# An attention and feed-forward kernel on one core: another order and other senders at the head of each batch element, and four banks for half of the score tiles by key

## What is computed

```python
def bi_wkv(r, k, v, w, u, time_emb):          # two of them: one before attention, one before the FFN
    tf = sigmoid(sum(time_emb, -1))
    decay = exp(-exp(w)) * (0.5 + 0.5 * tf)
    ek = exp(minimum(k, 30)); ekv = ek * v
    nf, df = scan(a = a * decay + ekv_t), scan(b = b * decay + ek_t)      # over the tokens
    nb, db = the same scans in reverse
    euk = exp(minimum(u + k, 30))
    num = nf + nb - ekv + euk * v
    den = df + db - ek + euk
    return sigmoid(r) * num / maximum(den, 1e-8) * (0.8 + 0.2 * tf)

def attention(h, w_qkv, w_o):                 # 16 heads of 32, causal, softmax over the keys
    q, k, v = split(h @ w_qkv.T)
    probs = softmax(where(causal, q @ k.T / sqrt(32), min))
    return (probs @ v) @ w_o.T

def ffn(x, w_gate, w_up, w_down):             # inputs and weights quantized in blocks of 32
    return mx(silu(mx(x) @ mx(w_gate).T) * (mx(x) @ mx(w_up).T)) @ mx(w_down).T

x = x + attention(bi_wkv(x, fside, fside, w1, u1, cond), w_qkv, w_o)
x = x + ffn(bi_wkv(x, fside, fside, w2, u2, cond), w_gate, w_up, w_down)
```

## Time and profile before

| | us |
|---|---|
| median of 3 runs | 870.95 (870.93 to 872.39) |
| the profiled execution | 873.02 |
| its span | 871.3 |
| DVE busy | 752.6 (86%) |
| PE busy | 741.5 (85%) |
| ACT busy | 507.6 (58%) |

### The profile page before, as it was taken

How to read it: one execution, slowest core, us unless ns; L and a number is a source line. 1 busy time by engine, 2 the same in 40 slices (tenths; PEclk the granted TensorE clock), 3 DMA queues, 4 the chain that set the end, 5 groups by cost and what they waited for, 6 DMA issues and landing times.

```text
span 871.3 us, 10845 instructions
## 1 busy us (share of the span) xinstructions
PE 741.5 (85%) x3964; PEld 393.8 (45%) x4001; DVE 752.6 (86%) x1070; ACT 507.6 (58%) x754; POOL 72.6 (8%) x149
## 2 busy tenths in 40 slices
PE   4567668699889999798899998988899998999785
PEld 1222223355544444454444443555444444557674
DVE  4899999999999879789998798899898888834887
ACT  4966655376874575378764663677736636443440
POOL 1000001202000003011000021110000211200000
PEclk9786687899999999999999999999999999999998
DMA  9623210557100005654010047460100355500001
GB/s 325 266 96 109 101 63 23 125 124 182 39 30 21 1 12 128 190 163 102 13 37 1 13 97 205 113 166 14 37 1 12 83 153 135 126 1 1 1 2 48
DMA packets 31252, 73.06 MB, mean 84 GB/s; under 512 B 5856, under 2 KB 6880, under 8 KB 29408
## 3 DMA queue, kind: packets, MB, share of 16 engines
q1 hardware_dynamic: 19584, 46.67, 17.9%
q0 software_dynamic: 6144, 16.79, 8.1%
q10 hardware_dynamic: 5472, 8.92, 3.2%
HBM read 34.61 MB, written 4.19 MB: 45 GB/s over the span
## 4 chain that ended last, share of the span: by engine, by line
DVE 44%; PE 26%; issue 13%; ACT 8%; DMA 3%; SPq 3%; POOL 1%; ACTq 0%; DVEq 0%
PE bank L1627 9%; DVE negmax L1077 5%; DVE num L983 3%; SPq L337 3%; PE bank L1520 2%; DVE fn L969 2%; PE bank L1464 2%; PE bank L1482 2%; PE bank L1392 2%; ACT region L583 2%; DVE ratio L1116 2%; PE bank L1426 2%; PE bank L1493 2%; DMA stacks<-rows 1%; DVE den L994 1%
## 5 line engine op out<-in xcount | busy, mean ns | idle before, releaser
L1077 DVE TENSOR_REDUCE negmax<-bank 128x4 f32<-128x512 f32 (+2 forms) x96 | 97.8, 1036 | 31.9 <-PE bank L1429 19.5
L583 ACT ACTIVATE region<-bank 128x384 f32<-128x384 f32 (+1 forms) x192 | 93.2, 526 | 46.3 <-PE bank L1467 45.4
L1464 PE MATMUL bank<-stacks 128*128 128x512 f32 (+3 forms) x256 | 103.2, 411 | 18.8 <-ACT region L583 13.4
L1400 PE MATMUL bank<-h,wqkv 128*128 128x512 f32 x256 | 115.5, 605 | 0.0
L1426 PE MATMUL bank<-stacks 128*128 128x128 f32 (+3 forms) x256 | 78.6, 402 | 7.1 <-DVE negmax L1077 4.9
L337 POOL DMA_DIRECT2D stacks<-rounded_rows x64 | 34.7, 550 | 521.1 <-DVE ratio L1116 321.6
L1400 PEld LDWEIGHTS bank<-h,wqkv 128*128 128x128 f32 x256 | 49.4, 195 | 58.1 <-issue 57.2
L1466 PE MATMUL bank<-maxrow,pick 128*128 128x384 bf16 (+3 forms) x236 | 73.2, 310 | 0.0
L1464 PEld LDWEIGHTS bank<-stacks 128*128 128x128 f32 x256 | 50.3, 197 | 45.0 <-ACT region L583 27.4
L1392 PE MATMUL bank<-wqkv,h 128*128 128x512 f32 x128 | 62.7, 635 | 4.7 <-DVE h L1017 4.7
L1682 PE MATMUL bank<-region,ident 128*128 128x512 f32 x64 | 49.2, 930 | 12.0 <-DVE identb L928 12.0
(11 more groups left out here) (197 smaller groups left out, 1558.5 us busy)
## 6 DMA issues: line engine op xcount, KB each, us to landing
stacks<-rounded_rows SPq DMA_DIRECT2D x64, 128.0 KB, 4.5
stacks<-rounded_rows POOLq DMA_DIRECT2D x64, 128.0 KB, 5.0
stacks<-rows SPq DMA_DIRECT2D x64, 128.0 KB, 2.5
stacks<-rows POOLq DMA_DIRECT2D x64, 128.0 KB, 2.6
kt<-in_fside ACTq DMA_DIRECT2D x30, 256.0 KB, 3.3
region<-in_w_gate SPq DMA_DIRECT2D x4, 1024.0 KB, 11.3
h<-in_x SPq DMA_DIRECT2D x4, 1024.0 KB, 5.7
xt<-in_x SPq DMA_DIRECT2D x4, 1024.0 KB, 5.6
```

The source lines that it names most:

```text
L583: nc.scalar.activation(probs[:, i, P_AT[tiles[0]]:P_AT[tiles[0]] + columns], key_bank(g, n)[:, 0:columns], ACT.Exp, scale=SCALE).then_inc( ...
L1077: nc.vector.tensor_reduce(o, scored, AX_X, ALU.max, negate=True).then_inc(max_taken, 1)
L1400: mm = nc.tensor.matmul(qk_banks(g)[s][:, :], wqkv[:, j, C * s + P * g:C * s + P * g + P], h[:, j, :], start=(j == 0), stop=(j == CJ - 1))
L1464: nc.tensor.matmul(o, ks[s][:, i, P * t:P * t + P], qs[s][:, i, P * t:T], start=True, stop=False, skip_group_check=True)
```

## The change

Six edits. **(1)** Head 1 of group 1 is stacked by ACT instead of SP, in all four turns, behind `low_parts`; SP sends head 0 alone, and does so ahead of the stores of the element before, which follow it. **(2)** DVE at the head: the xt additions go ahead of `add_own(b, 9)`, `forward(b, 2, ...)` behind the fourth maximum. **(3)** PE at the head: the first projection is cut in two halves around slots 0 and 1, the second stands behind slots 2 and 3, the values behind slots 4 and 5. **(4)** ACT: `copy_maxima(b, 0)` ahead of the two `weigh`, `copy_values(b, (0,))` behind the first two exponentials; a table load ahead of `load_k` and `floored`; `cap_exp(b, 7)` behind the twelfth exponential of group 3 instead of the ninth. **(5)** Score tiles by key of groups 1 and 2 go from the fifth on (n of 4 or more) round banks 4, 5, 6, 7 instead of 4, 5 (HALF_RING is 4). **(6)** Unit 6, the first on bank 6, waits for `normed`, units 8 to 11 for the exponential of the unit four before.

```diff
-            return bank[(4, 5, 0, 1, 2, 3)[n % 6]] if g == GROUPS - 1 else bank[4 + n % 2]
+            if g == GROUPS - 1:
+                return bank[(4, 5, 0, 1, 2, 3)[n % 6]]
+            return bank[4 + (n % 4 if g and n >= HALF_RING else n % 2)]
...
@@ block.sync @@
             def turn(b, more):
                 sp.wait_ge(down_ready, 1 + b)
-                stack(sp, b, 1, 0, 2)
+                stack(sp, b, 1, 0, 1)
                 if b:
+                    store(b - 1, True)
                     sp.wait_ge(stored, b * (16 * CJ))
                     sp.dma_start(xt[:, :, :], x[b]).then_inc(x_in, 16)
...
@@ block.scalar @@
             def turn(b, more):
                 high_parts(b, 1)
                 low_parts(b, 1)
+                act.wait_ge(down_ready, 1 + b)
+                stack(act, b, 1, 1, 2)
                 load_k(b, 1)
                 reciprocals(b, 1)
                 own_exp(b, 2)
                 copy_raw(b, 2)
                 late_high_parts(b)
+                copy_maxima(b, 0)
                 weigh(b, 2, 0)
                 weigh(b, 2, 1)
-                copy_maxima(b, 0)
+                exps(b, 0, 0, 2)
                 copy_values(b, (0,))
-                exps(b, 0, 0, 5)
+                exps(b, 0, 2, 5)
...
-                exps(b, 3, 2, 9)
+                exps(b, 3, 2, 12)
                 cap_exp(b, 7)
-                exps(b, 3, 9, 12)
...
@@ block.tensor, scores_by_key @@
+                elif g and HALF_RING <= n:
+                    free = n - 2 if n == HALF_RING + 1 or n == HALF_RING else n - 4
+                    if n == HALF_RING + 2:
+                        pe.wait_ge(normed, b * GROUPS + g)
+                    if n not in (HALF_RING + 2, HALF_RING + 3):
+                        pe.wait_ge(p_ready, b * (GROUPS * UNITS) + g * UNITS + free + 1)
```

More of the change, by code:

```diff
@@ L379, in turn, with store @@
                     stack(sp, b + 1, 0, 0, 2)
+            def store(b, more):
                 for j in range(CJ):
@@ L392, in _ @@
                 turn(b, b + 1 < B)
+            store(B - 1, False)
             sp.wait_ge(weights_in, 32)
@@ L673, in turn @@
                 copy_maxima(b, 2)
+                if more:
+                    table(6)
                 load_k(b, 4)
                 floored(b, 4)
-                if more:
-                    table(6)
                 exps(b, 2, 0, 1)
@@ L1231, in turn @@
             def turn(b, more):
[L1232 to L1241, removed]
+                maxima(b, 0, 0)
+                maxima(b, 0, 1)
+                if b == 0:
                     backward(b, 1, 1)
                     add_own(b, 1)
[L1244 to L1247, removed]
+                maxima(b, 0, 2)
+                maxima(b, 0, 3)
+                forward(b, 2, 0)
+                forward(b, 2, 1)
                 maxima(b, 0, 4)
@@ L1373, in turn @@
                 backward(b, 9, 1)
-                add_own(b, 9)
                 for j in range(CJ):
@@ L1377, in turn @@
                     nc.vector.tensor_tensor(xt[:, j, :], bank[j][:, :], xt[:, j, :], ALU.add).then_inc(out_ready, 1)
+                add_own(b, 9)
             for b in range(B):
@@ L1395, in project_values, with project_qk @@
                     mm.then_inc(v_ready, 1)
-            def project_qk(b, g, s):
-                for j in range(CJ):
+            def project_qk(b, g, s, first=0, last=CJ):
+                for j in range(first, last):
                     mm = nc.tensor.matmul(qk_banks(g)[s][:, :], wqkv[:, j, C * s + P * g:C * s + P * g + P], h[:, j, :],
-                                          start=(j == 0), stop=(j == CJ - 1))
-                mm.then_inc(qk_ready, 1)
+                                          start=(j == 0), stop=(j == CJ - 1), skip_group_check=True)
+                if last == CJ:
+                    mm.then_inc(qk_ready, 1)
             def leave_low(b, g, s):
@@ L1733 @@
 VALUE_ORDER = (2, 3, 0, 1)
+HALF_RING = 4
 SLOT_BEHIND = ({1: 0, 2: 1, 4: 2, 7: 3, 9: 4, 11: 5}, {2: 2, 5: 3, 8: 4, 11: 5})
```

7 lines of the change are left out of this document (4 added, 3 removed).

## The result

| | before | changed | ratio |
|---|---|---|---|
| median of four runs each, same chip | 871.11 us (870.93 to 872.39) | 857.15 us (856.61 to 857.56) | 0.9836, 95% interval 0.9819 to 0.9853 |
| profiled execution | 873.02 us, span 871.3 | 857.56 us, span 855.8 | |
| a later chip, median of 9 and 4 runs | 873.13 us | 857.33 us (856.94 to 857.74) | 0.9818, 0.9804 to 0.9832 |

The kernel is 14 us faster by the first pair of medians and 15.8 us faster by the second; the two profiled spans differ by 15.5 us.

What follows compares the result with a forecast made beforehand. The prediction took the wait for SP's stacks to bound the heads and DVE to bound groups 1 to 3. Gains of 4.6 + 4.35 + (3.3 + 1.6) = 13.85 us off 870.95 gave 857.1 us, range 852.5 to 862.5.

Steps and rivals of the forecast that it cites:

- The sum of 13.85 us: Whole kernel: gains of 4.6 in b = 1, 4.35 in b = 2 and 3.3 + 1.6 in b = 3.
- The end of the last landing: Head of b = 1: group 1's last stack lands at 356.5 instead of 360.26, between 355.7 and 359.0.
- ACT's issues: Head: ACT issues four stacks at 0.6 us each, 2.4 us, with bounds of 2.3 to 10 us for four.
- The rival that the prediction put beside it: Heads: the bytes bound, last stack lands at 359.0, each head gives 1.3 to 1.7 less: 861.6 us, chance 0.16.
- Slot 4 of group 1: Head of b = 1: DVE reaches it at 373.5 instead of 378.69, PE being the later one; gain 5.2 us.
- The 0.6 us taken off b = 1: First slot of group 2: b = 1 would wait for PE as b = 2 does (0.57 us), leaving 4.6 us.
- The 1.15 us of `cap_exp`: Group 3 of b = 2: DVE's wait for the sum goes once `cap_exp` no longer stands between the exponentials, 1.15 us.
- The slow clock of b = 1: Behind b = 1's head: TensorE's clock at 0.50 in 366 to 368 goes; b = 2 and b = 3 have none.
- Four banks: Units 8 and 11 of two groups in the last turn find a free bank, 0.4 us each: 1.6 us.
- b = 0 at nothing: Turn b = 0: no stores, DVE is bound behind PE's first tile; gain 0, between -0.5 and +1 us.
- Copying the maxima first, at nothing: ACT: `copy_maxima` ahead of `weigh` moves work inside ACT's slack and gives nothing of its own.
- The slower rival: Heads: ACT's queue takes the place of SP's, issues of 2.50 us, last landing at 362.3: 875.6 us, chance 0.03.

Runs made afterwards that it cites:

- order alone: Changed kernel with the queues of before (stores first, then all eight of SP's stacks, none from ACT): 871.46 us, ratio 0.9987.
- queues alone: Kernel before with ACT sending head 1 of group 1 and SP's stack ahead of the stores, engines' order and two banks kept: 865.86 us, ratio 0.9920.

## Why the prediction was right, and where it wasn't

Forecast 857.1, measured 857.15. The agreement to 0.05 us is luck. The sum of 13.85 us was short of the 15.5 us by which the spans differ: for the profiled execution it gives 859.2 us, and that took 857.56, 1.6 less. The medians met because the three runs of before had theirs 2.1 us under the profiled execution, where the changed kernel has 0.4; the two errors cancelled. On the later chips the median of before was 872.7 to 873.1, and on the one of them that ran the changed kernel the gain was 15.8 us. The mechanism of the heads, from which most of the sum comes, is what the runs bear out.

**The end of the last landing** (356.5 out of 355.7 to 359.0): the landing released ACT at 356.50. Right, and the step on which most of the gain rests. The order alone gave nothing and the queues alone 6.9 us; together they gave 15.8. So about half of the gain comes only with both. Each takes one of two limits of the same stretch away: with the queues alone DVE still waits 5.82, 5.54 and 4.37 us in the three heads, with both 3.2 in each; with the order alone the landing holds it. That isn't the whole of it: the order alone also made the landing later, and of what the changed kernel has over the queues alone 1.6 us are the four banks. The prediction summed DVE's work against both limits at once, which is why it did not fall into this; the expectation of the order alone, which priced it as a part of the sum, did.

**ACT's issues** (0.6 us each, 2.4 for four): 3.08 us in b = 1, 0.74 at the median. Too low by a quarter, without effect. Whether ACT matters as a sender at all the prediction left open. The Trainium skill (DMA: Bandwidth & Descriptors, Issuing engines are not separate DMA queues) has it that several senders save only issuing time. With the stacks first, 857.46 against 857.33 us agrees. The rival that the prediction put beside it, 861.6 us, did not come: standing ahead of the stores was enough by itself for the early landing.

**Slot 4 of group 1.** Forecast 373.5 in b = 1, measured 373.54; the additions began at 344.57 instead of 344.95, the first tile by key came at 360.78 by the chain (forecast 360.5), and PE was the later one, as said. In b = 2, taking off what b = 1 had gained, 548.98 + 5.18 = 554.16 (forecast 554.0), in b = 3 724.41 + 10.23 = 734.64 (734.8).

**The 0.6 us taken off b = 1** for a wait at the first slot of group 2 (0.57 in b = 2): wrong. Neither b = 1 nor b = 2 has it; b = 3 has 0.32 us. So b = 1 gave 5.1 instead of 4.6, and b = 2 0.57 more. From turn to turn of these two kernels this wait lies between 0 and 0.57 us. What sets it, no run here was made to show.

**The 1.15 us of `cap_exp`** in b = 2: the wait went, with another of 0.21 us behind it. The step's mechanism was the failure. It took the wait for two ACT instructions in the way. The run with these put back shows a longer idle time of PE, 2.58 us instead of 1.42, in three turns, the low clock and the late sum behind it in two of them, and 4.5 us in the median. The mechanism had been in reach: the earlier trace rows put the wait in one turn of three, though the same two instructions stand in each.

**The slow clock of b = 1**, priced at 1.9 us in that head and said not to be in b = 2 and b = 3: the second profile of before has it in all three. In the first it stands in b = 3 too, a window that the prediction hadn't looked at; no row says what it cost there. Slot 4 of b = 3 gained 3.50 us by the change and that of b = 2 3.10, so at most some 0.4 us:

```profile
720.00:722.00 2.00, 1.23 (x5) 0.81 (x6) 1.90 (x6) 0.65 (x1) 0.00 (x0) 0.59 0.90 236
```

The changed kernel, whose PE has no idle time of over half a microsecond left in its heads, shows it in none of them in the two profiles taken; both have it elsewhere, in groups 1 to 3 of one turn (near 405 and near 581 us) and behind 790 us.

**Four banks**, 4 x 0.4: 5.08 - 3.50 = 1.58 us in b = 3, and 1.6 by the run with two banks. Right.

**b = 0 at nothing**: 0.07 by this pair of profiles, 1.63 by the second pair, where the kernel before had its late sum (1.15 us) in b = 0. So it is borne out only to about half a microsecond. PE waits 0.62 us for `normed` at unit 6 there (0.7 forecast), covered by DVE as said. **Copying the maxima first, at nothing**: right, by its run.

**The slower rival** needed landings past 360.3 us. The run with the stores ahead of SP's stack shows that such landings come with ACT as sender (`late_high_parts` starts at 363.68 in b = 1), by way of SP's issues behind the stores (8.95 us for four) and not of ACT's (4.07 us); even then the median stayed 4 us below that of before.

## What to carry to other kernels

A transfer that the next stage waits for goes ahead of the stores in its queue, where what waits for these is less pressing (here SP's load of xt): with the stores first ACT's step came 3.2 to 6.5 us later in each head, whoever sent the stacks. Where a stretch has two limits close together (a landing, and the order of two engines' work), taking away one can show little (here nothing for one, 6.9 us of 15.8 for the other); try both before dropping either. A short ACT instruction between PE's inputs is to be priced by the idle time that it gives PE, not by its own length.

## What was not expected of the hardware

- The same DMA issue on SP takes 0.70 us when the queue begins with it (2.79 for four). Behind four stores of 256 KB it takes 1.06 us where SP alone issues beside POOL (8.50 for eight) and 2.2 us where ACT issues too (8.95 for four, stores first). The stores themselves take 2.4 to 3.9 us for four at the front of the queue, 7.85 behind four stacks of SP and four of ACT, and 2.1 to 2.7 behind eight of SP, which took 7.3 to 7.6 themselves. That would fit an issuing engine that is held while earlier bytes are under way; no run here was made to show it. The time of issuing is not small beside the transfer there (3.46 us for the last landing of the order alone).
- TensorE's clock fell behind an idle time of 2.58 us in five of twelve turns: in one of three in each of two executions of the kernel before and in the queues alone, and in two of three with `cap_exp` put back. Behind 1.42 us at the same place it fell in none of thirty. The same program gives either, and a DVE wait of 1.15 us comes and goes with it.
